# Layer norm moved from VectorE to ScalarE, with a bias per token made on GpSimd, in a kernel whose four queues are laid out in advance

## What is computed

```python
def _layernorm(x, axis=-1, eps=1e-05):
    m = jnp.mean(x, axis=axis, keepdims=True)
    v = jnp.var(x, axis=axis, keepdims=True)
    return (x - m) / jnp.sqrt(v + eps)

# in a layer of the stack:
    h = (h - mu) / jnp.sqrt(var + 1e-05) * lg + lb
    h = h @ w1 + b1
    a, g = jnp.split(h, 2, axis=-1)
    h = a * jax.nn.gelu(g, approximate=False)
    x = x + h @ w2 + b2
```

## Time and profile before

| | |
|---|---|
| median of 3 runs | 1702.99 us (1702.83 to 1704.13) |
| the profiled execution's own time | 1691.46 us |
| its span, first to last instruction | 1689.7 us |
| instructions | 48659 |
| busy: PE, DVE, ACT, POOL | 1513.6, 1446.1, 1325.0, 1202.3 us |
| TensorE's mean granted clock | 0.966 of full speed |

### The profile page before, as it was taken

How to read it: one execution, slowest core, us unless ns; L and a number is a source line. 1 busy time by engine, 2 the same in 40 slices (tenths; PEclk the granted TensorE clock), 3 DMA queues, 4 the chain that set the end, 5 groups by cost and what they waited for, 6 DMA issues and landing times.

```text
span 1689.7 us, 48659 instructions
## 1 busy us (share of the span) xinstructions
PE 1513.6 (90%) x17754; PEld 1219.8 (72%) x17754; DVE 1446.1 (86%) x3170; ACT 1325.0 (78%) x3908; POOL 1202.3 (71%) x1290
## 2 busy tenths in 40 slices
PE   5798998999988999899899979989898989998997
PEld 3576777666776777777677867768786776777886
DVE  8888788887989699889988879788998887879896
ACT  3598888577876897887888876978785866978995
POOL 8999685349765768777888847788836553889880
PEclk8899999998999999999999999999998997999999
DMA  5110122100210021012010030011031040010010
GB/s 141 40 30 11 26 58 81 62 21 11 65 52 23 11 71 33 20 32 62 14 27 20 21 100 15 21 27 30 14 113 37 20 119 27 21 29 23 12 24 17
DMA packets 49637, 66.77 MB, mean 40 GB/s; under 512 B 8146, under 2 KB 32252, under 8 KB 49404
## 3 DMA queue, kind: packets, MB, share of 16 engines
q1 hardware_dynamic: 49404, 63.66, 13.9%
HBM read 22.75 MB, written 15.73 MB: 23 GB/s over the span
## 4 chain that ended last, share of the span: by engine, by line
PE 27%; POOL 25%; DVE 22%; ACT 16%; issue 8%; DMA 0%; SPq 0%; POOLq 0%; ACTq 0%; DVEq 0%
ACT bank L1336 9%; POOL sums L1265 9%; POOL parts L1256 7%; PE bank L1739 6%; POOL parts L1269 6%; DVE parts L1654 5%; DVE neg_full L1533 4%; PE bank L1971 3%; PE bank L1877 3%; PE bank L1789 2%; PE bank L1926 2%; DVE neg_max L1533 2%; PE bank L1887 2%; PE bank L1837 2%; PE bank L1954 2%
## 5 line engine op out<-in xcount | busy, mean ns | idle before, releaser
L1256 POOL TENSOR_TENSOR parts<-parts 128x512 f32<-128x512 f32 x256 | 327.8, 1288 | 188.6 <-DVE parts L1654 187.7
L1265 POOL TENSOR_TENSOR sums<-sums,neg_half 128x8 f32<-128x8 f32 x256 | 426.6, 1666 | 21.3
L1336 ACT ACTIVATE bank<-bank,neg_max 128x128 f32<-128x128 f32 x1024 | 361.6, 388 | 40.0 <-DVE neg_max L1533 39.2
L1654 DVE TENSOR_TENSOR parts<-bank,rope 128x1024 f32<-128x1024 f32 x256 | 308.9, 1216 | 42.1 <-ACT squares L1403 40.2
L1269 POOL TENSOR_TENSOR parts<-parts,sums 128x512 f32<-128x512 f32 x256 | 267.8, 1046 | 37.0 <-POOL sums L1265 0.5
L1336 ACT ACTIVATION_READ_ACCUMULATOR bank<-bank,neg_max 128x1 f32 x1024 | 259.9, 255 | 0.0
L1403 ACT ACTIVATE squares<-bank 128x512 f32<-128x512 f32 x256 | 159.5, 629 | 57.2 <-PE bank L1739 35.9
L1971 PE MATMUL bank<-ident,parts 128*128 128x128 f32 x1024 | 164.9, 286 | 43.6 <-POOL parts L1269 34.4
L1739 PE MATMUL bank<-wqkv_hi,h_hi 128*128 128x512 f32 x384 | 183.8, 479 | 15.0 <-DVE probs L1569 5.9
L1837 PE MATMUL bank<-ident,probs 128*128 128x128 f32 x1024 | 157.9, 282 | 37.4 <-DVE probs L1569 31.9
L1569 DVE TENSOR_TENSOR probs<-bank,prob_inv 128x512 f32<-128x512 f32 x256 | 177.0, 691 | 8.8
(11 more groups left out here) (147 smaller groups left out, 3823.5 us busy)
## 6 DMA issues: line engine op xcount, KB each, us to landing
between<-val SPq DMA_DIRECT2D x192, 128.0 KB, 2.4
laid_dram<-halves SPq DMA_DIRECT2D x96, 128.0 KB
stacked_q<-laid_dram SPq DMA_DIRECT2D x16, 512.0 KB, 6.3
stacked_k<-laid_dram SPq DMA_DIRECT2D x16, 512.0 KB, 3.4
x_sb<-in_L_attn_x_dram SPq DMA_DIRECT2D x16, 128.0 KB, 3.1
out_dram<-x_sb SPq DMA_DIRECT2D x16, 128.0 KB, 1.8
laid_dram<-plain SPq DMA_DIRECT2D x8, 128.0 KB
raw_qkv<-in_L_ffn_wqkv_dram SPq DMA_DIRECT2D x3, 256.0 KB, 4.2
```

What stands on the lines that cost most here:

```text
L1256: nc.gpsimd.tensor_tensor(joined, joined, sines[:, :, ::-1], ALU.add).then_inc(sems["rope_joined"], 1)
L1265: nc.gpsimd.tensor_tensor(sums[:, u], sums[:, u], neg_half[:], ALU.pow).then_inc(sems["pool_step"], 1)
L1336: last = nc.scalar.activation(scores, scores, ACT.Exp, bias=neg_max[:, u, row:row + 1], accum_out=prob_sum[:, u, row:row + 1])
L1654: nc.vector.tensor_tensor(parts[:, u].rearrange("p o (h d) -> p o h d", d=LOCAL_D), bank[:].rearrange("p (o h d) -> p o h d", o=1, d=LOCAL ...
```

## The change

The normalising goes from VectorE to ScalarE: `normal = Identity(rstd * source + shift)` with a scale and a bias for each token. GpSimd makes the bias, shift = -mean * rstd, in two operations: it negates the mean ahead of the epsilon addition, and multiplies by rstd after the power. The step NORM is ordered, and its semaphore counted, on ScalarE. The small tensors of a sequence share one buffer. The lengths in PASSES and all due times that the layout works from are new, so the order on every queue is another one. The diff without most of these tables:

```diff
@@ PASSES
-    "SPLIT": [(ACTE, 0.27), (DVE, 0.47)], "WO": [(PE, 1.65), (DVE, 0.88)],
-    "LNH": [(PE, 0.24), (DVE, 0.69), (POOL, 1.04)], "LNX": [(DVE, 0.7), (POOL, 1.06)], "NORM": [(DVE, 0.68)],
+    "SPLIT": [(ACTE, 0.38), (DVE, 0.53)], "WO": [(PE, 1.65), (DVE, 0.88)],
+    "LNH": [(PE, 0.24), (DVE, 0.69), (POOL, 1.55)], "LNX": [(DVE, 0.7), (POOL, 1.57)], "NORM": [(ACTE, 0.72)],
...
-STRETCH = 2.4003
-PATIENCE = (0.0, 0.0, 0.143, 0.722)
+STRETCH = 2.3829
+PATIENCE = (0.106, 0.0, 0.146, 0.767)
...
@@ emits
-        "LNH": [{}, {"vector_step": 1, "var_ready": 1}, {"pool_step": 1, "rstd_ready": 1}],
-        "LNX": [{"vector_step": 1, "var_ready": 1}, {"pool_step": 1, "rstd_ready": 1}],
+        "LNH": [{}, {"vector_step": 1, "var_ready": 1}, {"pool_step": 2, "rstd_ready": 1}],
+        "LNX": [{"vector_step": 1, "var_ready": 1}, {"pool_step": 2, "rstd_ready": 1}],
@@ COUNTED: "normed" from VectorE's names to ScalarE's
@@ buffers
-        mean_var = per_stream("mean_var", [P, TILES, 2])
-        var_eps = per_stream("var_eps", [P, TILES])
-        rstd = per_stream("rstd", [P, TILES])
+        moments = per_stream("moments", [P, 5, TILES])
+        mean_var = [x[:, 0:2].rearrange("p m t -> p (m t)").rearrange("p (t m) -> p t m", m=2) for x in moments]
+        var_eps, rstd, shift = [[x[:, n] for x in moments] for n in range(2, 5)]
+        shift = shift * ROUNDS
@@ GpSimd, norm_scale
                 pool.wait_ge(sems["var_ready"], count("var_ready", step))
+                nc.gpsimd.tensor_scalar(shift[s][:], mean_var[s][:, :, 0], -1.0, None, ALU.mult)
                 nc.gpsimd.tensor_scalar(var_eps[s][:], mean_var[s][:, :, 1], EPS, None, ALU.add).then_inc(sems["pool_step"], 1)
+                pool.wait_ge(sems["pool_step"], count("pool_step", step, 1))
+                nc.gpsimd.tensor_tensor(rstd[s][:], var_eps[s][:], neg_half[:, 0:TILES], ALU.pow).then_inc(sems["pool_step"], 1)
                 pool.wait_ge(sems["pool_step"], count("pool_step", step))
-                nc.gpsimd.tensor_tensor(rstd[s][:], var_eps[s][:], neg_half[:, 0:TILES], ALU.pow).then_inc(sems["rstd_ready"], 1)
+                nc.gpsimd.tensor_tensor(shift[s][:], shift[s][:], rstd[s][:], ALU.mult).then_inc(sems["rstd_ready"], 1)
@@ ScalarE (VectorE's normalise and its call are taken out)
+            def normalise(step):
+
+                s, before = step[1], last_step({"LNH", "LNX"}, step)
+                act.wait_ge(sems["rstd_ready"], count("rstd_ready", before))
+                for t in range(TILES):
+                    source = banks[BANK_OF[before]][:, P * t:P * (t + 1)] if before[0] == "LNH" else x_sb[s][:, t]
+                    last = nc.scalar.activation(normal[s][:, t], source, ACT.Identity, bias=shift[s][:, t:t + 1],
+                                                scale=rstd[s][:, t:t + 1])
+                last.then_inc(sems["normed"], 1)
```

More of the change, by code:

```diff
@@ L127 @@
 PASSES = {
[L128 to L129 removed]
+    "SPLIT": [(ACTE, 0.38), (DVE, 0.53)], "WO": [(PE, 1.65), (DVE, 0.88)],
+    "LNH": [(PE, 0.24), (DVE, 0.69), (POOL, 1.55)], "LNX": [(DVE, 0.7), (POOL, 1.57)], "NORM": [(ACTE, 0.72)],
     "LNT": [(PE, 0.27), (ACTE, 0.3), (DVE, 0.34)], "STATE": [(PE, 0.3), (ACTE, 0.79)],
[L131 to L132 removed]
+    "W1": [(PE, 0.75), (ACTE, 0.36), (DVE, 0.4)], "W2": [(PE, 1.34), (DVE, 1.01)], "OT": [(PE, 0.24), (ACTE, 0.28)], "WOF": [(PE, 0.45), (DVE, 0.36)],
+    "XB": [(POOL, 0.75)], "MT": [(DVE, 0.51), (PE, 0.45), (DVE, 0.6)], "Y": [(ACTE, 0.49)],
     "XADD": [(PE, 0.28), (DVE, 0.34)], "VAL": [(PE, 0.75), (ACTE, 0.49)], "VALF": [(PE, 0.66), (ACTE, 0.28)],
[L134 to L135 removed]
+    "Q": [(PE, 0.81), (ACTE, 0.49), (DVE, 1.13), (DVE, 0.6), (POOL, 1.29), (POOL, 3.17)], "R": [(PE, 0.4), (ACTE, 0.49)],
+    "QF": [(PE, 0.85), (ACTE, 0.72), (DVE, 0.79)], "T": [(PE, 0.44), (ACTE, 0.49)]}
 HANDOVER = (0.2, 0.16, 0.12, 0.08)
@@ new lines @@
+START_AT = (-93.6, -135.0, -480.4, -239.9, 5.9, 15.6, 144.0, 337.7, 1101.8, 1154.6, 829.9, 870.1, 1120.5, 969.1,
+            579.8, 1119.6)
+STRETCH = 2.3829
+PATIENCE = (0.106, 0.0, 0.146, 0.767)
+DUE = {('E', 0, True): 42.1, ('FOLD', 0, False): 193.68, ('FOLD', 1, False): -358.45, ('LNH', 0, False): -228.05,
+       ('LNH', 1, False): -221.75, ('LNH', 2, False): -101.09, ('LNT', 0, False): 73.76, ('LNT', 1, False): 237.75,
+       ('LNT', 2, False): 5.54, ('LNX', 0, False): -129.04, ('LNX', 1, False): 305.17, ('MASKS', 0, False): 259.38,
[13 rows of a table added]
@@ new lines @@
+PHASE_DUE = {0: 184.38, 1: -40.93, 2: 163.23, 3: -477.48, 4: -84.38, 5: -147.39, 6: -29.82, 7: -127.41, 8: 203.35, 9:
+             -214.83, 10: 78.91}
+LATER = {(0, 0): 21.4, (0, 1): 1085.57, (0, 2): 298.89, (0, 3): -25.51, (0, 4): 195.74, (0, 5): 189.3, (0, 6): 172.7,
[26 rows of a table added]
+NUDGE = {('E', 0, 5, 0): -5.56, ('E', 0, 5, 1): 1103.45, ('E', 0, 5, 4): -10.62, ('E', 0, 5, 5): -18.36, ('E', 1, 5,
[3 rows of a table added]
+         -240.92, ('LNH', 3, 2, 0): 621.87, ('LNH', 4, 2, 0): -1.87, ('LNH', 11, 4, 0): 696.47, ('LNH', 12, 10, 0):
+         813.73, ('LNT', 1, 10, 0): -1382.58, ('LNT', 2, 4, 0): 544.77, ('LNT', 7, 10, 0): 163.76, ('LNT', 10, 4, 1):
+         681.96, ('LNT', 11, 8, 0): -858.2, ('LNT', 11, 10, 0): 633.29, ('LNT', 13, 4, 0): 122.66, ('LNT', 14, 2, 0):
+         106.99, ('LNT', 15, 4, 0): -36.73, ('LNX', 8, 4, 0): 350.27, ('LNX', 14, 0, 0): 371.67, ('MT', 0, 5, 0):
[28 rows of a table added]
+         ('SPLIT', 9, 2, 0): -680.59, ('SPLIT', 9, 8, 0): 273.47, ('STATE', 3, 6, 0): 206.27, ('STATE', 14, 6, 0):
[7 rows of a table added]
+         ('V', 14, 9, 1): 847.01, ('VAL', 2, 8, 0): -36.68, ('VAL', 4, 6, 1): -390.82, ('VAL', 5, 8, 0): 11.21,
+         ('VAL', 5, 8, 1): 353.3, ('VAL', 6, 6, 0): -308.42, ('VAL', 7, 6, 1): -294.52, ('VAL', 11, 8, 0): -21.9,
+         ('VAL', 13, 8, 0): -398.64, ('VAL', 14, 8, 1): -608.27, ('VALF', 11, 4, 0): -553.94, ('VALF', 13, 4, 0):
[12 rows of a table added]
+         ('X', 15, 7, 2): -392.72, ('XADD', 2, 10, 0): 341.78, ('XADD', 3, 10, 0): 614.84, ('XADD', 5, 10, 0):
+         -498.87, ('Y', 4, 5, 1): 4.76, ('Y', 4, 5, 9): 16.88, ('Y', 6, 5, 7): 455.93, ('Y', 11, 5, 7): 207.32, ('Y',
+         15, 5, 1): 3.62}
@@ L294, in passes @@
     if kind == "X":
-        return [(DVE, 0.61)] if is_full(ph) else [(DVE, 0.61), (ACTE, 1.38), (DVE, 0.83)]
+        return [(DVE, 0.61)] if is_full(ph) else [(DVE, 0.63), (ACTE, 1.38), (DVE, 0.83)]
     if kind == "V":
@@ L895 @@
            ("probs_ready", "turned_copied", "heads_copied", "heads_plain", "state_set", "high_ready", "squares_ready",
-            "values_ready", "full_values", "qk_ready", "gelu_ready", "high_parts", "exps_ready", "heads_merged"),
-           ("max_ready", "vector_step", "probs_scaled", "heads_scaled", "state_ready", "var_ready", "normed", "max_split",
+            "values_ready", "full_values", "qk_ready", "normed", "gelu_ready", "high_parts", "exps_ready", "heads_merged"),
+           ("max_ready", "vector_step", "probs_scaled", "heads_scaled", "state_ready", "var_ready", "max_split",
             "max_added", "split_ready", "hidden_ready", "x_ready", "squares_summed", "rope_parts", "halves_ready",
@@ L1443, in _ @@
                     copy_heads(step)
+                elif step[0] == "NORM":
+                    normalise(step)
                 elif step[0] == "SPLIT":
@@ L1601, in layer_norm @@
                 last.then_inc(sems["var_ready"], 1)
-            def normalise(step, source):
-                s = step[1]
-                dve.wait_ge(sems["rstd_ready"], count("rstd_ready", last_step({"LNH", "LNX"}, step)))
-                for t in range(TILES):
-                    last = nc.vector.tensor_scalar(normal[s][:, t], source[t], mean_var[s][:, t, 0:1], rstd[s][:, t:t + 1],
-                                                   ALU.subtract, ALU.mult)
-                last.then_inc(sems["normed"], 1)
             def add_to_state(s, bank, dst, bias):
@@ L1632, in dense @@
                     layer_norm(step, [x_sb[s][:, t] for t in range(TILES)])
-                elif kind == "NORM":
-                    before = last_step({"LNH", "LNX"}, step)
-                    if before[0] == "LNH":
-                        bank = banks[BANK_OF[before]]
-                        normalise(step, [bank[:, P * t:P * (t + 1)] for t in range(TILES)])
-                    else:
-                        normalise(step, [x_sb[s][:, t] for t in range(TILES)])
                 elif kind == "SPLIT":
```

24 lines of the change are left out of this document (removed), and 169 rows, old and new, of tables (DUE, LATER, NUDGE).

## The result

The changed kernel took 1711.46 us (median of 5 runs, 1708.29 to 1715.65), the kernel before 1702.83 us beside it (1697.62 to 1704.13). The ratio is 1.0059, 95% interval 1.0039 to 1.0079: slower, by 10 us by the ratio, and clear of no change. The forecast was 1695.5 us, faster. The time lies within its range, on the other side of no change.

What follows compares the result with a forecast made beforehand. TensorE's work bounds the kernel, plus holes the other three engines leave in it. Steady stretch -11.7, fill +4.3, end 0 sum to -7.4 us, taking 1703.0 to 1695.6, or 1695.5; range 1679 to 1714 us.

Steps and rivals of the forecast that it cites:

- The prices of the operations: Per norm: ScalarE pair 0.80 us, GpSimd negation 0.23 and product 0.23; 0.54 us more latency.
- VectorE ... -36% of 77.5: -28.2 us: Steady stretch, 160 to 1650 us: TensorE's waits for VectorE shrink 36% as VectorE's occupied share falls from 0.870 to 0.810.
- The order. I leave it at nothing: Rewritten due times reorder all four queues; nothing in the trace prices this, so counted as zero, only widening the range.
- the same rule: Rule of thumb for the steady stretch: waits for an engine go with its busy share over its idle share.
- The waits for ScalarE: Steady stretch: TensorE's waits for ScalarE grow 57% of 23.7 us, +13.5 us, to near 37.
- GpSimd's terms: Added GpSimd operations: +3.0 us of TensorE's waits in the steady stretch, +4.3 us in the pipeline's fill.
- The slower rival: ScalarE takes VectorE's place as what TensorE waits for; 1709 us half way, 1736 all the way; chance 0.24.
- The gain of ten switches: ScalarE's Exp/Gelu switches, 1.283 us each: ten fewer or more are 13 us of ScalarE, some 2 us of time.
- The wait for the power: VectorE's wait for GpSimd's power, 15.1 us in 20 waits, 13 us of it in the steady stretch, moves to ScalarE.

Runs made afterwards that it cites:

- VectorE less, old order: Kernel before, same queue order, with one normalising instruction over 8 columns per norm instead of two over 128; 1686.31 us, ratio 0.9937.
- ScalarE more, old order: Kernel before, same queue order, with two unread 128x32 Identity activations added on ScalarE where each norm is due; 1716.08 us, ratio 1.0116.
- ScalarE more, new order: Changed kernel without its GpSimd operations, plus two unread 128x32 Identity activations ahead of each normalising; 1730.84 us, 1.0201 to the kernel before, 1.0204 to that without them.
- GpSimd more in the norm's path, old order: Kernel before, same order, normalising still on VectorE, with the negation and product added on GpSimd ahead of the normalising, result unused; 1738.45 us, ratio 1.0239.
- GpSimd more behind it, old order: Kernel before, same order, with two unused GpSimd operations per norm added behind the one that releases the normalising; 1723.49 us, ratio 1.0163.
- GpSimd less, old order: Kernel before, same order, without GpSimd's epsilon addition, the power reading the variance directly; 1676.64 us, ratio 0.9885.
- the two GpSimd operations, new order: Changed kernel (ratio 1.0059) against itself without the negation and product, bias being the mean (1695.66 us, ratio 0.9997); both ratios to the kernel before.
- old order, the move without GpSimd's part: Kernel before with normalising moved to ScalarE, other steps in their old order, no added GpSimd operations, bias the mean; 1719.91 us, ratio 1.0136.
- new order, without the move: Changed kernel's queues with normalising put back on VectorE and without the two GpSimd operations; 1744.43 us, ratio 1.0285 to the kernel before.
- new order, the move without GpSimd's part: Changed kernel in its own order without the two GpSimd operations, bias the mean; 1695.66 us, ratio 0.9997 to the kernel before.
- The floor of 128x8: Floor under the sums of squares moved from GpSimd to VectorE: on the changed kernel 1815.36 us, 1.0680; on the kernel before 1769.04 us, 1.0421.

## Why the prediction was wrong

What a microsecond of work was worth on each engine, as the change of the time over the change of the page's busy time:

| | work, us | time, us | us per us |
|---|---|---|---|
| VectorE less, old order | -39.2 | -10.7 | 0.27 |
| ScalarE more, old order | +60.2 | +19.7 | 0.33 |
| ScalarE more, new order | +60.6 | +34.6 | 0.57 |
| GpSimd more in the norm's path, old order | +47.5 | +40.6 | 0.85 |
| GpSimd more behind it, old order | +49.9 | +27.7 | 0.56 |
| GpSimd less, old order | -29.6 | -19.5 | 0.66 |
| the two GpSimd operations, new order | +46.5 | +10.5 | 0.23 |

(Times are ratio less 1, times 1698 us, each give or take some 4 us, so 0.27 and 0.33 are not told apart. Work in the fifth and sixth row: GpSimd's page 1252.2 and 1172.7 us.)

TensorE's waits from 160 to 1650 us by the engine that they are put down to, in the prediction's own terms (a slower kernel has done a little less of its work by 1650 us):

| | VectorE | ScalarE | GpSimd | ratio |
|---|---|---|---|---|
| before | 77.5 | 23.7 | 18.4 | 1 |
| forecast | 49.3 | 37.2 | 21.4 | |
| changed kernel | 71.2 | 39.0 | 15.7 | 1.0059 |
| old order, the move without GpSimd's part | 72.0 | 46.5 | 16.7 | 1.0136 |
| new order, without the move | 106.2 | 23.6 | 11.6 | 1.0285 |
| new order, the move without GpSimd's part | 74.0 | 40.1 | 10.4 | 0.9997 |
| old order, VectorE less | 67.7 | 25.3 | 24.1 | 0.9937 |
| old order, ScalarE more | 79.7 | 34.2 | 16.9 | 1.0116 |

Point by point, by the prediction's steps:

- *The prices of the operations* held. The pair on ScalarE took 0.84 to 0.91 us against 0.80, the product 0.20 against 0.23, the negation 0.24 against 0.23. The added latency of a norm came to 0.58 us against 0.54, since the two added operations brought two gaps and not one. The estimate of 0.865 us for the pair, from the Trainium skill's figures ("ScalarE: Activation LUTs", "What ACT_TABLE_LOAD costs"), was nearer than mine.
- *The step that failed is "VectorE ... -36% of 77.5: -28.2 us", with the order left at nothing.* TensorE's waits for VectorE were to fall to 49 us; they stayed at 71.2, and at 74.0 without the GpSimd operations. Of the two terms, -28.2 and +13.5, the sum is -14.7; measured for move and order together it is -0.5 us (0.9997), give or take 3. The forecast change was -7.4 us and the measured one +10.0, and 14.2 of these 17.4 us are here.
- *What the runs show in its place* depends on the order. In the old order, from whose rows the term was worked out, the move takes 5.5 us off the waits for VectorE, not 28.2, adds 22.8 to those for ScalarE, not 13.5, and costs 23 us. In the new order the move takes off 32.2 and adds 16.5, near the forecast's two terms, and gains 49 us; but that order begins with 106.2 us of waits for VectorE and is 2.85% slower without the move. The one gain and the other loss come to zero. *"The order. I leave it at nothing"* was therefore not a small omission: what the move is worth can't be told apart from the order in which it is made.
- *Why the relief counts for so little in the old order* is in part open. Relief of VectorE alone does pay: -10.7 us (-6.8 to -14.6) where the same rule gives -15.3, for 46 us of groups. Load on ScalarE alone is what the rule has wrong: +19.7 us where it gives +6.5 (60.2 us, of which 0.89 in the steady stretch; +28% of 23.7). These two prices, for 69.4 us less and 70.6 us more, would make +4 us of the move in the old order; measured are +23. That ScalarE's lateness reaches TensorE under VectorE's name, through the exps, squares and splits, would explain part, and VectorE's waits for ScalarE rose by 52.8 us in the change. But they also rose by 19.5 us where only VectorE's work was cut, and load on ScalarE alone added no more than 2.2 us to TensorE's waits for VectorE. The rest may lie in where the norms stand in ScalarE's queue, which in that run waited 16.1 us for GpSimd ahead of work that others need; no run moved them.
- *The waits for ScalarE*, forecast 37 us, came out at 39.0, in part by luck: in the order for which the figure was worked out they are 46.5.
- *GpSimd's terms*, +3.0 in the steady stretch and +4.3 in the fill, 7.3 us, came out at 10.5, give or take 4, in the new order, so right within the noise. In the old order the same two operations cost 40.6. That order was laid out without them, and the lateness grows all along the kernel, where the forecast had 3.0 us for the steady stretch. A busy share of 71% did not tell which of the two it would be.
- *The slower rival*, ScalarE in VectorE's place, had the sign and not the mechanism: it was to decide once TensorE's waits for ScalarE pass 45 us, and the kernel was slower at 39.0. What tipped it was GpSimd's two operations.
- *The gain of ten switches* happened (20 loads fewer) and lies within the 0.9997.
- *The wait for the power*, 13 us in the steady stretch by proportion, was there to be read: it is 9.8 us in 16 waits of the 20. That moves the sum by 0.2 us. The row of the kernel before, from 160 to 1650 us:

```profile
DVE normal L1607 <- POOL rstd L1248: 9.8, 16, 1.3
```

Still open: whether a layout as well fitted as the one before exists for the changed kernel. ScalarE's price in the new order, 0.57 against 0.33, says that it has less room there, but no run here searched for another order. No run here computes the whole reference and beats the kernel before: the two below it by more than noise leave out most of the normalising, or epsilon.

## What to carry to other kernels

Where the order of every queue is fixed in advance, the busy share of an engine is no measure of its room. The same 47 us on GpSimd, idle for 29% of the time, cost 40.6 us in an order laid out without them and 10.5 us in one laid out with them. A move of work from one engine to another cost 23 us in one order and gained 49 in the other. So price the edit and the order together, as a two by two of runs: old and new work, each in the old and the new order. And price a load by a run that adds or removes a known amount of it in place, with the order held, before arguing from shares or from the engine that a wait is put down to.

## What the hardware showed beyond that

A small VectorE operation from SBUF to SBUF can be held up for several times its own length, by one kind of GpSimd instruction and not by another. In the run with VectorE's relief the normalising works on 8 columns; from a bank and from x_sb:

```profile
L1609 DVE TENSOR_SCALAR normal<-bank,mean_var,rstd x64: 272/280/288, 77.9 to 1670.9; 128x8 f32<-128x8 f32 x64
L1609 DVE TENSOR_SCALAR normal<-x_sb,mean_var,rstd x48: 259/291/1245, 10.5 to 1514.0; 128x8 f32<-128x8 f32 x48
```

From a bank it takes 272 to 288 ns, from SBUF 259 to 1245, 506 on average, more than the 478 that 128 columns took in the kernel before. That is part of why the relief was smaller than meant. The floor of 128x8, also in SBUF, took 170 ns at its shortest and 416 in the median, 127.6 us for 256 instead of the 38 that I had meant. Its trace in the old order shows what holds it. Two floors in the timeline, one that starts during GpSimd's rope sum (L1256) and one during its power (L1262):

```profile
38.36 1.28 POOL L1256 TENSOR_TENSOR parts<-parts 128x512 f32<-128x512 f32 x1
38.54 1.13 DVE L1661 TENSOR_SCALAR sums<-sums 128x8 f32<-128x8 f32 x1
```

```profile
49.41 1.64 POOL L1262 TENSOR_TENSOR sums<-sums,neg_half 128x8 f32<-128x8 f32 x1
49.97 0.17 DVE L1661 TENSOR_SCALAR sums<-sums 128x8 f32<-128x8 f32 x1
```

The first ends with the rope sum, the second runs at its own length. Of all 256, 144 took 230 ns or more, and each of these ended 24 to 34 ns after the end of a rope sum (L1256) or a rope scaling (L1266). The 49 that started under the power, itself 1.65 us long, took 170 to 210 ns, and the 36 that met no GpSimd instruction at their start 170 to 173. The kernel before shows the same with the normalising from x_sb: 22 of 96 took 500 ns or more, and 21 of these ended 81 to 86 ns after a rope sum or a rope scaling; the 15 that started under the power took 332 to 346. From a bank none of 128 took more than 414, though 45 started under the rope sum. So here VectorE waits, from SBUF only, until the rope sum or the rope scaling has ended. The Trainium skill says ("SBUF — State Buffer", "Who interferes with whom") that a VectorE operation in a two-port mode and a GpSimd instruction exclude each other, and that whichever comes first has the shared ports for its whole instruction. The trace agrees for the rope sum and the rope scaling. For the power it does not: none of the 49 floors was held until its end.
